# Leaving out the second half of short expert blocks, by a list, and moving the last odd block's output into the loop

## The chip, the cores and the metric

The kernel runs on one core of a Trainium2 chip. The metric is the device time of one execution in microseconds (us). Five engines work side by side, each with its own instruction queue: PE (matrix products; PEld, its weight loads, is listed apart), DVE (vector arithmetic), ACT (functions and copies), POOL (here: gathers, scatters and small loads through its DMA queue) and SP (transfers). They wait for one another through semaphores. An instruction that waits holds up everything behind it in its engine's queue.

## What is computed

Four layers on a tensor of 2048 tokens of 256 numbers, each adding an expert network's output to its input. Layers 0 to 2 are the ones in question:

```python
# layer 0: every token goes to the experts that hold the first 0.8 of the router's probability
h = relu(einsum('bth,ehf->betf', x, W1) + b1)      # 8 experts, 256 -> 1024
y = einsum('betf,efh->beth', h, W2) + b2           # 1024 -> 256
out = einsum('bte,beth->bth', gate, y)
# layer 1: every token goes to the expert of the largest logit, 256 -> 1024 -> 256, gelu
# layer 2: the same, 256 -> 512 -> 256, gelu
x = x + out
```

The router decides on the chip which tokens an expert gets. With the given inputs the tokens for each of the eight experts are 1250, 991, 1681, 916, 1881, 989, 825, 1662 in layer 0; 0, 0, 0, 0, 0, 1, 2046, 1 in layer 1; and 402, 238, 116, 124, 331, 278, 335, 224 in layer 2.

## The kernel before

**Blocks.** Each expert's tokens are sorted into blocks of 256 rows, that is two tiles of 128 rows; an expert's last block is filled up with rows that are dumped. That makes 43 blocks in layer 0, 10 in layer 1 and 12 in layer 2, 65 in all. A block is short when its second tile holds no token: an expert whose last block has 128 tokens or fewer. By the counts above these are blocks 27, 35 and 42 of layer 0 (42 is the last one, and 43 is odd), blocks 0 and 9 of layer 1 (9 is the last of an even number) and blocks 3, 4, 6, 8 and 10 of layer 2.

**What PE does with a block** (`blocks(L)`). `trans` turns the gathered rows, four transposes. `hidden` makes the hidden layer for both tiles at once, 256 columns wide; each product is three matmuls (lines 821 to 823) of a high and a low part, 48 matmuls in layers 0 and 1 and 24 in layer 2. `output` makes the second product, one tile of 128 tokens after the other (j = 0, 1): 24 matmuls for each tile in layers 0 and 1, 12 in layer 2.

**What the others do.** POOL gathers a block's rows (L711) and scatters the result, through L739 in layer 0 (`scatter_add`, which first waits at L723 until the scatter of the block before has landed) and through L729 in layers 1 and 2. ACT evaluates the hidden layer (L1435, L1436). DVE makes all low parts (L1671): of the first weights (`w1_lo`), the second weights (`w2_split`), the hidden layer (`lows`) and the block's inputs (`x_lo`); it then adds the bias to each output tile (`outputs`, L1938) and in layer 0 multiplies it by the gate (L1943).

**The order.** Blocks q = 2i + k go through a hardware loop over i with k = 0 and 1 written out in its body, one block of lookahead, and the loop's length fixed for the worst routing: iterations past the end are skipped by a branch (L956). Within iteration i PE's order is: hidden(i,1), trans(i+1,0), output(i,0), hidden(i+1,0), trans(i+1,1), output(i,1). So what follows output(q) on PE is the hidden layer of block q + 2, and its first matmul waits for x_lo(q + 2). DVE's order is: w1_lo of q + 2, w2_split and lows of q + 1, x_lo of q + 2, then outputs of q. An odd last block is left over: its second product stands behind the loop, after the skipped iterations, on PE (`output(pairs, 0)`) and on DVE (`outputs(pairs, 0)`).

**The lists.** The routing is turned into block and slot lists by a chain of small DVE operations, each waiting for the one before (`link`). It ends for the gathers with the list of slots (L1830), on which the first gather waits. PE, ACT, DVE, POOL and SP each read the number of blocks with a register load from SBUF (L417).

Of the kernel before, what the change touches and what calls it, by code (L numbers as in the profile page):

```python
# [67 lines left out]
def build(nc, t):  # L68

    with ExitStack() as ctx:  # L70
        def sb(name, shape, dt=F32):
            return ctx.enter_context(nc.sbuf_tensor(name, shape, dt))
# [52 lines left out]
        GBK = sb("block_gates", [P, 2, BTT])  # L125
        B2B = sb("b2_block", [P, 2, D])
        BLK = [sb(f"blocks{L}", [1, 64], I32) for L in SPARSE]


        ROWS = B * SEQ + DUMPS * P  # L130
# [687 lines left out]
        def _(pe):  # L818
# [88 lines left out]
            def blocks(L):  # L907
                NF = LAYERS[L][1] // P

                def trans(i, k):  # L910

                    first = isinstance(i, int) and i == 0
                    pe.wait_ge(s_xb[L][k], i * (16 * BTT) + 16 * BTT)
                    if not first:
                        pe.wait_ge(s_xlo[L], i * 2 + k - 1)
                    for m in range(KD):
                        for tt in range(BTT):
                            last = nc.tensor.transpose(PS[:, 6 + k, m * BT + tt * P:m * BT + (tt + 1) * P],  # L918
                                                       XBL[L][:, k, tt, m * P:(m + 1) * P], ident[:])
                    last.then_inc(s_xps[L], 1)  # L920

                def hidden(i, k, first=False):
                    q = i * 2 + k
                    pe.wait_ge(s_xlo[L], q + 1)
                    pe.wait_ge(s_w1sp[L], q + 1)
                    for f in range(NF):
                        if first and f == NF // 2:
                            trans(0, 1)
                        if not first or f >= 4:
                            pe.wait_ge(s_hhi[L], NF * q + (H0[L] + f - 3))  # L930
                        out = PS[:, f % 4, (f // 4) * BT:(f // 4 + 1) * BT]
                        for m in range(KD):
                            w = slice((m * NF + f) * P, (m * NF + f + 1) * P)
                            last = mm3(out, WB1[L][0][:, k, w], WB1[L][1][:, k, w], XTh[:, k, m, :], XTl[:, k, m, :],
                                       m == 0, m == KD - 1)
                        last.then_inc(s_hps[L], 1)

                def output(i, k):
                    q = i * 2 + k
                    pe.wait_ge(s_w2sp[L], q + 1)  # L940
                    pe.wait_ge(s_hlo[L], NF // 2 * (q + 1) + H0[L])
                    for j in range(BTT):
                        pe.wait_ge(s_yev[L], BTT * q + j + 1)
                        for f in range(NF):
                            tok = slice((f % 2) * BT + j * P, (f % 2) * BT + (j + 1) * P)
                            w = slice(f * D, (f + 1) * D)
                            last = mm3(PS[:, 4 + j, 0:D], HTh[:, k, f // 2, tok], HTl[:, k, f // 2, tok],
                                       WB2[L][0][:, k, w], WB2[L][1][:, k, w], f == 0, f == NF - 1)
                        last.then_inc(s_y[L], 1)

                pe.wait_ge(s_list, L + 1)
                steps, pairs, n = counts(pe, L)
                trans(0, 0)
                hidden(0, 0, True)
                with pe.Fori(0, STEPS[L]) as i:
                    with pe.If(i < pairs):  # L956
                        hidden(i, 1)
                        with pe.If(i + 1 < steps):
                            trans(i + 1, 0)
                        output(i, 0)  # L960
                        with pe.If(i + 1 < steps):
                            hidden(i + 1, 0)
                            with pe.If(i + 1 < pairs):
                                trans(i + 1, 1)
                        output(i, 1)
                with pe.If(pairs < steps):
                    output(pairs, 0)

            def ffn3():
                fh, fl = FEAT[3]  # L970
# [690 lines left out]
        def _(dve):  # L1661
            steps_done = [0]

            def link(ins):

                steps_done[0] += 1
                ins.then_inc(s_dve, 1)
                dve.wait_ge(s_dve, steps_done[0])
# [85 lines left out]
            def order(L):  # L1754
# [4 lines left out]
                et = "p (e t) -> p e t"  # L1759
                tmp = SC[:, 2, 0:ET].rearrange("p (t e) -> p t e", e=8)  # L1760
                cmp = SC[:, 2, ET:ET + 64].rearrange("p (e k) -> p e k", k=8)
                own, upto, even = (SC[:, 2, 256 + 8 * k:264 + 8 * k] for k in range(3))
                dve.wait_ge(s_rank, L + 1)

                link(nc.vector.tensor_copy(tot.rearrange(et, e=8),
# [7 lines left out]
                link(nc.vector.tensor_reduce(own, cmp, axis=AX.X, op=ALU.add))  # L1773
                link(nc.vector.tensor_tensor_scan(upto, ONE[:, 0:8], own, 0.0, ALU.mult, ALU.add))
                block_list(L, upto)
                nc.vector.tensor_tensor(own, upto, own, ALU.subtract)
                link(nc.vector.tensor_tensor(off, cum, tot, ALU.subtract))
                link(nc.vector.scalar_tensor_tensor(off.rearrange(et, e=8), own.unsqueeze(2).broadcast_to([P, 8, NT]),
# [20 lines left out]
                for c in range(NC):  # L1799
# [2 lines left out]
                    nc.vector.tensor_tensor(OHL[:, n, :].rearrange("p t (a o) -> p t a o", o=2), lane.unsqueeze(1).broadcast_to(pairs),  # L1802
                                            SLOP[:, n, :].unsqueeze(2).broadcast_to(pairs), ALU.is_equal).then_inc(s_inv, 1)

            def block_list(L, upto):
                n = BLOCKS[L]
                hit = SC[0:1, 6, 0:n * 8].rearrange("p (b e) -> p b e", e=8)
# [10 lines left out]
            def slot_tokens(L):  # L1818
# [3 lines left out]
                if L == 0:  # L1822
# [5 lines left out]
                                             empty.rearrange("p (g j) -> p g j", j=DUMPS),  # L1828
                                             DUMP[:].unsqueeze(1).broadcast_to([P, S // DUMPS, DUMPS]), ALU.mult))
                nc.vector.scalar_tensor_tensor(TOK[:, 0:S], inv, -1.0, empty, ALU.add, ALU.add).then_inc(s_tok, 1)  # L1830

            def order0():

# [3 lines left out]
                tot, cum, off = (SC[:, 5, k * ET:(k + 1) * ET] for k in range(3))  # L1837
                tmp = SC[:, 2, 0:ET].rearrange("p (t e) -> p t e", e=8)
                cmp = SC[:, 2, ET:ET + 64].rearrange("p (e k) -> p e k", k=8)
                own, upto, first = (SC[:, 2, 256 + 8 * k:264 + 8 * k] for k in range(3))  # L1840
                dve.wait_ge(s_rank, 1)
                link(nc.vector.tensor_copy(tot.rearrange(et, e=8),
                                           PS[:, 7, ET:2 * ET].rearrange("p (t e) -> p e t", e=8)))
# [17 lines left out]
                link(nc.vector.tensor_tensor(first, upto, own, ALU.subtract))  # L1861
                link(nc.vector.tensor_scalar(TGT, first[0:2 * LC], float(BTT), PIDC[0:2 * LC, 1:2], ALU.mult, ALU.add))
                link(nc.vector.tensor_copy(TGTB[:], TGT.unsqueeze(2).broadcast_to([2 * LC, 8, 2])))

                def columns(h):
                    T = NT // 2
# [32 lines left out]
            def blocks(L):  # L1899
# [67 lines left out]
                else:  # L1967
                    w2_lo(0, 0)
                with dve.Fori(0, STEPS[L]) as i:
                    with dve.If(i < pairs):  # L1970
                        with dve.If(i + 1 < steps):
                            w1_lo(i * 2 + 2, 0)
                        w2_split(i, 1)
                        lows(i * 2 + 1, 1)
                        with dve.If(i + 1 < steps):
                            x_lo(i * 2 + 2, 0)
                        outputs(i, 0)
                        with dve.If(i + 1 < steps):
# [5 lines left out]
                            lows(i * 2 + 2, 0)  # L1984
                            with dve.If(i + 1 < pairs):
                                x_lo(i * 2 + 3, 1)
                        outputs(i, 1)
                        if L == 0:
                            with dve.If(i + 1 < pairs):
                                gate_column(i + 1, 1)  # L1990
                with dve.If(pairs < steps):
                    outputs(pairs, 0)

            def add_back(L, n0, dh, dl):

# [748 lines left out]
```

## Time and profile before

| | |
|---|---|
| time before, median of 3 runs | 1180.87 us (1180.74 to 1182.09) |
| time of the profiled execution | 1182.63 us |
| its span in the trace | 1181.0 us |
| PE busy | 1020.3 us (86%), 7745 matmuls |
| DVE busy | 911.6 us (77%) |
| ACT busy | 641.6 us (54%) |
| POOL busy | 552.1 us (47%) |
| layer 0, 43 blocks | 80 to 611 us of the span |
| layer 1, 10 blocks | 691 to 824 us |
| layer 2, 12 blocks | 858 to 960 us |

The profiled execution is 1.76 us above the median, and its span is 1.63 us shorter than its time. Times within the span are counted from its start. PE's column of busy time counts pipelined matmuls, so a PE that is always busy is one that is never left without a matmul. "PEclk" is the granted clock of PE as a share of 2.4 GHz; 0.50 is 1.2 GHz. A row of a window gives its start and end, its length, then busy time and instructions of PE, PEld, DVE, ACT and POOL, the granted clock, the busy share of the DMA engines and GB/s. A row of a sequencer's operation gives its duration in ns (least, median, most) and when the first and the last began. In a timeline, where a row gives start and duration, the bracket behind an instruction gives its engine's idle time ahead of it and what ended that. A name with q behind an engine (PEldq, POOLq) is that engine's sequencer: loads of registers, branches and waits.

### The profile page before, as it was taken

The numbers are of one execution on the slowest core, as the hardware profiler recorded it, in microseconds if no ns is written. First come the engines' busy times: TensorE is split into PE (matmuls) and PEld (weight loads), VectorE is DVE, ScalarE is ACT, GpSimd is POOL, SyncE is SP. The second block draws the span as 40 slices with busy tenths as digits, with TensorE's granted clock in tenths as the row PEclk, the third lists the DMA queues.
The fourth block names the chain that finished last, engine by engine and source line by source line (L and its number), as shares of the span: only waits on it lengthen the run. The fifth ranks groups of instructions, "written<-read, shape, count | busy, mean of one in ns | idle before, by whom it ended". The sixth has DMA issues, their size and how long they took to land.

```text
span 1181.0 us, 26183 instructions
## 1 busy us (share of the span) xinstructions
PE 1020.3 (86%) x7745; PEld 967.1 (82%) x7745; DVE 911.6 (77%) x1565; ACT 641.6 (54%) x1388; POOL 552.1 (47%) x370
## 2 busy tenths in 40 slices
PE   6249999999999999999959749999859958889896
PEld 5239999999999999999956549998659946778785
DVE  7877888888888888888828768785748854867795
ACT  4227676767677767777615547672357625223321
POOL 1312888888888888888620044642047620000000
PEclk9568999999999999999976769999889979989998
DMA  7346787878787878787531267652368753030202
GB/s 212 116 170 206 225 242 217 246 228 243 216 250 224 246 215 247 227 246 215 145 62 37 70 225 259 231 186 83 105 218 257 238 161 114 14 90 24 95 14 72
DMA packets 84376, 203.50 MB, mean 172 GB/s; under 512 B 16626, under 2 KB 58114, under 8 KB 70754
## 3 DMA queue, kind: packets, MB, share of 16 engines
q1 hardware_dynamic: 60242, 159.35, 40.2%
q0 software_dynamic: 24080, 43.53, 15.3%
q8 instruction: 22, 0.36, 0.1%
q14 instruction: 32, 0.26, 0.1%
HBM read 168.36 MB, written 34.49 MB: 172 GB/s over the span
## 4 chain that ended last, share of the span: by engine, by line
PE 69%; DVE 11%; DMA 8%; issue 5%; ACT 3%; POOL 2%; POOLq 1%; SPq 1%; DVEq 0%; ACTq 0%
PE ps L821 22%; PE ps L822 21%; PE ps L823 21%; DMA y_rows<-w_raw,slot_rows 2%; PE ps L918 2%; DMA z_tok<-in_L_w 1%; PE ps L833 1%; DVE featA_lo L1671 1%; DVE hidden_lo L1671 1%; POOL w_raw L711 1%; DMA w_raw<-z_rows,slot_rows 1%; DMA z_tok<-y_rows 1%; DMA scratch<-in_L_w 1%; DVE x_tok L2000 1%; DMA z_rows<-z_tok 1%
## 5 line engine op out<-in xcount | busy, mean ns | idle before, releaser
L1435 ACT ACTIVATE hidden_f<-ps,b_block 128x256 f32<-128x256 f32 x472 | 240.8, 510 | 182.4 <-PE ps L823 179.6
L711 POOL DMA_INDIRECT x_tok<-z_gate_rows,slot_rows x86 | 236.1, 2745 | 121.7 <-DVE block_gates L1954 66.0
L1436 ACT ACTIVATE hidden_hi<-ps,b_block 128x256 fp32r<-128x256 f32 x472 | 242.6, 514 | 0.0
L821 PE MATMUL ps<-w_hi,featA_hi 128*128 128x256 f32 (+1 forms) x708 | 203.1, 287 | 9.5 <-DVE scratch L2349 6.3
L821 PE MATMUL ps<-featB_hi,hidden_hi 128*128 128x256 f32 x696 | 199.3, 286 | 7.1 <-issue 3.6
L822 PE MATMUL ps<-w_lo,featA_hi 128*128 128x256 f32 (+1 forms) x708 | 202.6, 286 | 0.0
L823 PE MATMUL ps<-w_hi,featA_lo 128*128 128x256 f32 (+1 forms) x708 | 202.5, 286 | 0.0
L822 PE MATMUL ps<-featB_lo,hidden_hi 128*128 128x256 f32 x696 | 195.8, 281 | 0.0
L823 PE MATMUL ps<-featB_hi,hidden_lo 128*128 128x256 f32 x696 | 195.2, 280 | 0.0
L1671 DVE TENSOR_TENSOR hidden_lo<-hidden_f,hidden_hi 128x512 fp32r<-128x512 f32 x272 | 175.2, 692 | 14.6 <-ACT hidden_hi L1436 13.3
L739 POOL DMA_INDIRECT x_rows<-w_raw,slot_rows x86 | 141.7, 1648 | 44.8 <-issue 25.0
L821 PEld LDWEIGHTS ps<-w_hi,featA_hi 128*128 128x128 f32 (+1 forms) x708 | 137.3, 194 | 11.1 <-issue 7.1
L821 PEld LDWEIGHTS ps<-featB_hi,hidden_hi 128*128 128x128 f32 x696 | 131.8, 189 | 7.9 <-DVE hidden_lo L1671 4.1
L823 PEld LDWEIGHTS ps<-w_hi,featA_lo 128*128 128x128 f32 (+1 forms) x708 | 137.6, 194 | 0.2
L822 PEld LDWEIGHTS ps<-w_lo,featA_hi 128*128 128x128 f32 (+1 forms) x708 | 137.5, 194 | 0.2
L823 PEld LDWEIGHTS ps<-featB_hi,hidden_lo 128*128 128x128 f32 x696 | 131.9, 189 | 0.0
L822 PEld LDWEIGHTS ps<-featB_lo,hidden_hi 128*128 128x128 f32 x696 | 131.7, 189 | 0.0
L711 POOL DMA_INDIRECT w_raw<-z_rows,slot_rows x44 | 53.5, 1215 | 155.2 <-DVE slot_rows L1830 74.9
L1938 DVE TENSOR_TENSOR w_raw<-ps,b_block 128x256 f32<-128x256 f32 x130 | 53.9, 419 | 68.2 <-PE ps L823 64.0
L821 PE MATMUL ps<-w_hi,featB_hi 128*128 128x256 f32 x288 | 84.5, 293 | 9.4 <-DVE w_lo L1671 6.5
L1671 DVE TENSOR_TENSOR featA_lo<-scratch,featA_hi 128x2048 fp32r<-128x2048 f32 (+3 forms) x49 | 89.4, 1824 | 2.6 <-ACT featA_hi L1559 1.3
L729 POOL DMA_INDIRECT y_rows<-w_raw,slot_rows x44 | 59.7, 1357 | 61.7 <-DVE w_raw L1938 47.5
(479 smaller groups left out, 2561.3 us busy)
## 6 DMA issues: line engine op xcount, KB each, us to landing
scratch<-in_L_w SPq DMA_DIRECT2D x53, 1024.0 KB, 5.2
z_tok<-in_L_w SPq DMA_DIRECT2D x32, 1024.0 KB, 8.2
x_tok<-in_L_w SPq DMA_DIRECT2D x21, 1024.0 KB, 5.0
b_block<-in_L_ffn_b POOLq DMA_DIRECT2D x65, 128.0 KB, 6.4
z_tok<-y_rows SPq DMA_DIRECT2D x12, 512.0 KB, 5.5
z_tok<-in_L_w SPq DMA_DIRECT2D x12, 512.0 KB, 5.3
scratch<-in_L_w SPq DMA_DIRECT2D x12, 512.0 KB, 5.2
z_rows<-z_tok SPq DMA_DIRECT2D x8, 512.0 KB, 2.9
```

Source lines behind the costliest of these rows:

```text
L711: gp.indirect_dma_start(XBL[L][:, k, tt, :], None, ZD if L else ZD0, bass.IndirectOffsetOnAxis(ap=TOK[:, q * BTT + tt:q * BTT + tt + 1], a ...
L729: gp.indirect_dma_start(YD, bass.IndirectOffsetOnAxis(ap=TOK[:, q * BTT + tt:q * BTT + tt + 1], axis=0), YB[:, k, tt, :], None).then_inc(s ...
L739: gp.indirect_dma_start(XD, bass.IndirectOffsetOnAxis(ap=TOK[:, q * BTT + tt:q * BTT + tt + 1], axis=0), YB[:, k, tt, :], None, compute_op ...
L821: nc.tensor.matmul(out, lh, rh, start=first, stop=False)
L822: nc.tensor.matmul(out, lh, rl, start=False, stop=False)
L823: return nc.tensor.matmul(out, ll, rh, start=False, stop=last)
L833: last = nc.tensor.transpose(PS[:, g % 4, j * P:(j + 1) * P], src[:, c * TPC + j, k * P:(k + 1) * P], ident[:])
L918: last = nc.tensor.transpose(PS[:, 6 + k, m * BT + tt * P:m * BT + (tt + 1) * P], XBL[L][:, k, tt, m * P:(m + 1) * P], ident[:])
L1435: act.activation(HF[:, f // 2, part], ps, func, bias=b1)
L1436: act.activation(HTh[:, k, f // 2, part], ps, func, bias=b1).then_inc(s_hhi[L], 1)
L1671: return nc.vector.tensor_tensor(out, full, hi.bitcast(F32), ALU.subtract)
L1938: nc.vector.tensor_tensor(YB[:, k, j, :], PS[:, 4 + j, 0:D], B2B[:, k, :], ALU.add).then_inc(s_yev[L], 1)
```

## The change

Three things are changed in layers 0 to 2.

DVE makes a list that says for each block whether its second tile is empty. `short_ends`, two linked operations, stands in the middle of the chain that makes the lists; `short_blocks`, three operations, follows at its end.

On PE, `output` loads the block's entry of that list into a register between the first and the second tile. If the block is short, the 24 (or 12) matmuls of the second tile are left out and one matmul of the same form takes their place, which only raises the semaphore and gives DVE defined values to read. The wait for the second tile's buffer now stands ahead of the branch. The other engines do the same work for a short block as before.

The output of an odd last block stands in the loop, in the iteration in which only k = 0 exists, on PE and on DVE; what stood behind the loop goes.

The core of the diff (the arrangement of DVE's loop follows PE's):

```diff
@@ PE, output(i, k)
-                    for j in range(BTT):
-                        pe.wait_ge(s_yev[L], BTT * q + j + 1)
+
+                    def tile(j):
                         for f in range(NF):
 ...
                         last.then_inc(s_y[L], 1)
 
+                    pe.wait_ge(s_yev[L], BTT * q + 1)
+                    tile(0)
+                    short = pe.value_load(SHORT[0:1, bass.ds(q, 1)], min_val=0, max_val=1)
+                    pe.wait_ge(s_yev[L], BTT * q + 2)
+                    with pe.If(short < 1):
+                        tile(1)
+                    with pe.Else():
+                        nc.tensor.matmul(PS[:, 5, 0:D], HTh[:, k, 0, P:2 * P], WB2[L][0][:, k, 0:D],
+                                         start=True, stop=True).then_inc(s_y[L], 1)
@@ PE, the loop
                 with pe.Fori(0, STEPS[L]) as i:
-                    with pe.If(i < pairs):
-                        hidden(i, 1)
+                    with pe.If(i < steps):
+                        with pe.If(i < pairs):
+                            hidden(i, 1)
                         with pe.If(i + 1 < steps):
                             trans(i + 1, 0)
                         output(i, 0)
                         with pe.If(i + 1 < steps):
                             hidden(i + 1, 0)
+                        with pe.If(i < pairs):
                             with pe.If(i + 1 < pairs):
                                 trans(i + 1, 1)
-                        output(i, 1)
-                with pe.If(pairs < steps):
-                    output(pairs, 0)
+                            output(i, 1)
@@ DVE, the list
+            def short_ends(own, upto, count, slack):
+
+                link(nc.vector.scalar_tensor_tensor(slack[0:1].unsqueeze(2), own[0:1].unsqueeze(2), float(BT), count[0:1],
+                                                    ALU.mult, ALU.subtract))
+                link(nc.vector.scalar_tensor_tensor(SEND[:], slack[0:1], float(P), upto[0:1], ALU.is_ge, ALU.mult))
+
+            def short_blocks(L):
+
+                n = BLOCKS[L]
+                room = HF[0:1].rearrange("p a c -> p (a c)")
+                hit, any_ = room[:, 0:n * 8].rearrange("p (b e) -> p b e", e=8), room[:, n * 8:n * 9]
+                link(nc.vector.tensor_tensor(hit, SEND[:].unsqueeze(1).broadcast_to([1, n, 8]),
+                                             IO[0:1, 1:n + 1].unsqueeze(2).broadcast_to([1, n, 8]), ALU.is_equal))
+                link(nc.vector.tensor_reduce(any_, hit, axis=AX.X, op=ALU.add))
+                nc.vector.tensor_scalar(SHORT[:, 0:n], any_, 1.0, None, ALU.min)
```

In `order` (layers 1 and 2) `short_ends` stands right behind `block_list`, in `order0` (layer 0) behind the two operations that turn the first block of each expert into targets. `short_blocks` is the last statement of `slot_tokens`, behind the operation at L1830 that raises the gathers' semaphore.

## Rows read from the trace of the kernel before

**Rows 1.** The page, part 1: busy us (share of the span) and instructions

```profile
PE 1020.3 (86%) x7745; PEld 967.1 (82%) x7745; DVE 911.6 (77%) x1565; ACT 641.6 (54%) x1388; POOL 552.1 (47%) x370
```

**Rows 2.** Windows inside layers 0, 1, 2 (columns as told above)

```profile
106.00:594.00 488.00, 488.00 (x4130) 488.00 (x4129) 420.82 (x538) 343.67 (x780) 388.78 (x201) 1.00 0.75 226
694.00:821.00 127.00, 122.68 (x997) 122.24 (x996) 92.57 (x98) 80.73 (x186) 57.20 (x46) 0.96 0.62 207
858.00:957.00 99.00, 78.79 (x658) 76.88 (x656) 71.47 (x106) 59.68 (x137) 62.59 (x60) 0.94 0.70 218
```

**Rows 3.** Timeline: PE, block 27's second tile, next hidden; start us, duration

```profile
428.58 0.28 PE L821 MATMUL ps<-featB_hi,hidden_hi 128*128 128x256 f32 x1
...
431.38 0.28 PE L821 MATMUL ps<-w_hi,featA_hi 128*128 128x256 f32 x1
```

**Rows 4.** Timeline: DVE in the same stretch, x_lo

```profile
429.83 0.68 DVE L1671 TENSOR_TENSOR w_lo<-ps,w_hi 128x512 fp32r<-128x512 f32 x1
```

**Rows 5.** Timeline: x_lo and the matmul it releases, in layer 2

```profile
884.04 0.68 DVE L1671 TENSOR_TENSOR w_lo<-ps,w_hi 128x512 fp32r<-128x512 f32 x1
884.85 0.38 PE L821 MATMUL ps<-w_hi,featB_hi 128*128 128x256 f32 x1 [2.07 <-DVE w_lo L1671]
```

**Rows 6.** One line's sequencer instructions, L955, window 429 to 429.7 us

```profile
L955 PEldq ALU_OP  x1: 32/32/32, 429.3 to 429.3; - x1
```

**Rows 7.** The same view: L417 (register load), L956; timeline of PE at 858

```profile
L417 PEldq TENSOR_LOAD <-blocks x3: 301/308/483, 80.1 to 858.4; - x3
L417 PEldq FUSED_REGOPS  x3: 151/151/165, 80.6 to 858.7; - x3
L956 PEldq COMPARE_BRANCH  x7: 208/208/208, 594.9 to 599.3; - x7
857.98 0.96 PE L903 MATMUL ps<-hidden_f 128*128 128x32 bf16 x32
```

**Rows 8.** Windows after two pauses of PE; timeline row of the first

```profile
1088.53 0.39 PE L821 MATMUL ps<-featB_hi 128*128 128x256 f32 x1 [1.90 <-DVE featB_lo L1671]
1089.08:1092.49 3.41, 3.41 (x18) 3.41 (x17) 1.54 (x4) 0.95 (x3) 0.00 (x0) 0.50 0.00 0
884.85:888.30 3.45, 3.45 (x29) 3.45 (x30) 2.35 (x4) 2.91 (x7) 2.66 (x2) 1.00 0.80 266
```

**Rows 9.** End of layer 0: timelines of PE, DVE, POOL; L723's waits

```profile
600.20 0.38 PE L821 MATMUL ps<-featB_hi,hidden_hi 128*128 128x256 f32 x1 [3.56 <-issue]
608.02 0.61 DVE L1943 TENSOR_SCALAR w_raw<-w_raw,block_gates 128x256 f32<-128x256 f32 x2
609.38 1.54 POOL L739 DMA_INDIRECT x_rows<-w_raw,slot_rows  x1 [7.54 <-DVE w_raw L1943]
L723 POOLq EVENT_SEMAPHORE  x2: 17/17/17, 594.6 to 604.1; - x2
```

**Rows 10.** Layer 1, block 0: timelines of DVE (x_lo of block 2), PE

```profile
717.09 0.68 DVE L1671 TENSOR_TENSOR w_lo<-ps,w_hi 128x512 fp32r<-128x512 f32 x1
...
720.29 0.28 PE L821 MATMUL ps<-w_hi,featB_hi 128*128 128x256 f32 x1
```

**Rows 11.** End of layer 1: timeline of POOL, block 9's scatters

```profile
818.90 0.96 POOL L729 DMA_INDIRECT y_rows<-w_raw,slot_rows  x1 [1.92 <-DVE w_raw L1938]
821.77 0.96 POOL L729 DMA_INDIRECT y_rows<-w_raw,slot_rows  x1 [1.92 <-DVE w_raw L1938]
```

**Rows 12.** Layer 2: timeline of POOL, one scatter

```profile
908.60 1.34 POOL L729 DMA_INDIRECT y_rows<-w_raw,slot_rows  x1 [3.15 <-DMA y_rows<-w_raw,slot_rows]
```

**Rows 13.** The lists: timelines of DVE (layer 0) and POOL (layer 1)

```profile
60.67 0.17 DVE L1860 TENSOR_TENSOR_SCAN scratch<-ones,scratch 128x8 f32<-128x8 f32 x1
60.88 0.17 DVE L1861 TENSOR_TENSOR scratch<-scratch 128x8 f32<-128x8 f32 x1
88.37 0.69 DVE L1671 TENSOR_TENSOR w_lo<-ps,w_hi 128x512 fp32r<-128x512 f32 x1 [5.01 <-ACT w_hi L1420]
687.68 1.03 POOL L711 DMA_INDIRECT w_raw<-z_rows,slot_rows  x1 [74.90 <-DVE slot_rows L1830]
```

More of the change, by code:

```diff
@@ L127, in build @@
         BLK = [sb(f"blocks{L}", [1, 64], I32) for L in SPARSE]
+        SHORT = sb("short_blocks", [1, 56], I32)
+        SEND = sb("short_block_end", [1, 8])
         ROWS = B * SEQ + DUMPS * P
@@ L1761, in order @@
                 cmp = SC[:, 2, ET:ET + 64].rearrange("p (e k) -> p e k", k=8)
-                own, upto, even = (SC[:, 2, 256 + 8 * k:264 + 8 * k] for k in range(3))
+                own, upto, even, slack = (SC[:, 2, 256 + 8 * k:264 + 8 * k] for k in range(4))
                 dve.wait_ge(s_rank, L + 1)
@@ L1775, in order @@
                 block_list(L, upto)
+                short_ends(own, upto, count, slack)
                 nc.vector.tensor_tensor(own, upto, own, ALU.subtract)
@@ L1830, in slot_tokens @@
                 nc.vector.scalar_tensor_tensor(TOK[:, 0:S], inv, -1.0, empty, ALU.add, ALU.add).then_inc(s_tok, 1)
+                short_blocks(L)
             def order0():
@@ L1839, in order0 @@
                 cmp = SC[:, 2, ET:ET + 64].rearrange("p (e k) -> p e k", k=8)
-                own, upto, first = (SC[:, 2, 256 + 8 * k:264 + 8 * k] for k in range(3))
+                own, upto, first, slack = (SC[:, 2, 256 + 8 * k:264 + 8 * k] for k in range(4))
                 dve.wait_ge(s_rank, 1)
@@ L1863, in order0 @@
                 link(nc.vector.tensor_copy(TGTB[:], TGT.unsqueeze(2).broadcast_to([2 * LC, 8, 2])))
+                short_ends(own, upto, count, slack)
                 def columns(h):
@@ L1969, in blocks @@
                 with dve.Fori(0, STEPS[L]) as i:
-                    with dve.If(i < pairs):
+                    with dve.If(i < steps):
                         with dve.If(i + 1 < steps):
                             w1_lo(i * 2 + 2, 0)
-                        w2_split(i, 1)
-                        lows(i * 2 + 1, 1)
+                        with dve.If(i < pairs):
+                            w2_split(i, 1)
+                            lows(i * 2 + 1, 1)
                         with dve.If(i + 1 < steps):
@@ L1986, in blocks @@
                                 x_lo(i * 2 + 3, 1)
[L1987 to L1992, printed above, removed]
+                        with dve.If(i < pairs):
+                            outputs(i, 1)
+                            if L == 0:
+                                with dve.If(i + 1 < pairs):
+                                    gate_column(i + 1, 1)
             def add_back(L, n0, dh, dl):
```

## The prediction

> **What bounds the kernel now.** I read the busy totals first and distrust them: PE is busy 86% of the span, the most of all [rows 1], but that is an average over stages with different limits. So I went on to windows inside each layer. In layer 0 PE is never without a matmul: 488.00 of 488.00 us at clock 1.00, 4130 matmuls, so 0.118 us each [rows 2]. In layer 1 PE is busy 97% and DVE 73%; in layer 2 PE 80%, DVE 72%, POOL 63%, and nobody is full [rows 2]. A product left out can therefore save its time in layer 0 and 1 at most, and only as far as the next thing on PE is ready. Which thing that is, I read from timelines around single short blocks, since that is where the change acts.
>
> **Part 1: second products left out.** A second tile is 24 matmuls, one of them replaced: 23 x 0.118 = 2.71 us freed on PE per short block of layers 0 and 1, and 11 x 0.118 = 1.30 in layer 2.
>
> *Layer 0, blocks 27 and 35.* Block 27's second tile starts at 428.58 and the next hidden layer at 431.38 [rows 3]. That hidden layer needs x_lo(29), which DVE does at 429.83 for 0.68, so until 430.51 [rows 4]. From the end of such an operation to the matmul that waited for it passes 884.85 - (884.04 + 0.68) = 0.13 us [rows 5]. So it can start at 430.64: the gain is 431.38 - 430.64 = 0.74 us, not 2.71.  Block 35 has the same pattern (the hidden layer 0.75 later than x_lo allows). Together 1.48; the bounds are 0 and 2 x 2.71 = 5.42.
>
> *Layer 1, block 0.* x_lo(2) ends at 717.09 + 0.68 = 717.77, plus 0.13 = 717.90; the hidden layer starts at 720.29 [rows 10]. Gain 2.39, nearly all of 2.71, because DVE is ahead here.
>
> *Layer 1, block 9, the last.* Nothing follows on PE; what follows is its second scatter. It began at 821.77, released by DVE's addition; the first began at 818.90 for 0.96 [rows 11]. With the second tile there at once, POOL can issue it behind the first: 818.90 + 0.96 + 0.30 (gap between issues) = 820.16. Gain 1.61.
>
> *Layer 2, five blocks.* POOL's scatters wait for the scatter before to land, 3.15 us in the row shown and alike three more times [rows 12], and PE waits 2.07 us for x_lo [rows 5]. PE stops early only to wait longer: gain 0. Bounds: +5 x 1.30 = 6.5 gained if PE leads after all, -5 x 0.21 = -1.0 if each jump shows [rows 7]. I take 0, by the row of POOL.
>
> **Part 2: the load and the branch on PE.** Each of 65 blocks gains a register load (0.31 for the load, 0.15 for the register operation behind it, up to 0.05 between them and an assert), a wait and a branch of 0.07 to 0.21 [rows 7]: about 1.05 us of sequencer time with the enclosing branches. It stands in front of the second tile, so PE's queue must hold more than that. The loop's back edge, which stands behind the last matmul of an iteration, was executed at 429.3 while those matmuls ran until 431.3 [rows 6, 3]: the sequencer is 2.0 us ahead. 1.05 fits, so I cost it at nothing; its cover is the queue of matmuls in front. If that cover is gone, each of the 53 blocks of layers 0 and 1 pays up to 1.05. The buffer wait that now stands before the branch is long satisfied in layer 0: DVE emptied that bank for the block before, and a hidden layer of 48 x 0.118 = 5.7 us lies between. Nothing else is queued behind it but PE's own next matmuls.
>
> **Part 3: the odd last block's output in the loop.** Before, PE walks 7 skipped iterations (branch at L956, seven of them from 594.9 to 599.3) and sits idle 3.56 us before block 42's output at 600.20; DVE's gates run at 608.02 for 0.61, and the scatter starts at 609.38 [rows 7, 9]. After, output(42) follows block 41's at once. PE ends 600.20 - 3.56 = 596.64; 24 matmuls x 0.118 = 2.8 make 599.5; addition and gates end by 601. Block 42 is short, so its second tile is there too. Then what is late next? The scatter must wait until block 41's has landed, which was at 604.1 [rows 9]. From the end of DVE's gates, 608.63, to the scatter's start passed 0.75; 604.1 + 0.75 to 0.9 gives 605.0. Gain 609.38 - 605.0 = 4.4 us. The second scatter and the reloading of rows behind it follow in a fixed chain. The skipped iterations now lie behind the output, under the scatter. Bounds 0 (block 41's landing is not earlier and something else waits) and 5.
>
> **Part 4: the list.** Linked operations on 8 numbers follow each other every 60.88 - 60.67 = 0.21 us [rows 13]. short_ends adds two, 0.42, to the chain that ends in the slot list. In layer 0 DVE goes through it without a gap; in layer 1 POOL's gather waited for exactly that list [rows 13]: +0.42 each. In layer 2 the gather waits for rows from DMA: 0. short_blocks (three operations, the first on 352 numbers; at the 0.69 us that 512 columns take it is at most 1.4 in all) comes behind the gather's release, in front of DVE's 5.01 us of waiting for ACT [rows 13]: 0; without that cover, 1.4.
>
> **The sum.** +0.42 + 0.42 - 1.48 - 2.39 - 1.61 - 4.4 + 0 = -9.0 us. On the profiled execution 1182.6 becomes 1173.6; on the median, 1180.87 - 9.0 = **1171.8**.
>
> **The rivals.**
>
> *The clock falls in the pauses.* Blocks 27 and 35 leave PE about 2.71 - 0.74 = 2.0 us without work, in a stage that so far had none. A pause of 1.90 us ahead of 1088.53 was followed by 3.41 us at 0.50, that is 1.2 GHz; the pause of 2.07 ahead of 884.85 was followed by clock 1.00 [rows 8, 5]. So it can go either way. At half clock 3.41 us do the work of 1.7: if both fall, 3.4 us are lost and the time is 1175.2. [...]
>
> *The end of layer 0 does not move*, because the reload of rows waits on something other than block 42's scatter: 1171.8 + 4.4 = 1176.2.
>
> *PE bounds everywhere.* Then all products left out count: 5 x 23 + 5 x 11 = 170 x 0.118 = 20.1 us, less 0.84 for the list: 1161.6. For it speaks PE's 86% [rows 1]; against it x_lo, done only at 430.51 [rows 4]. The Trainium skill (Perfetto Trace Analysis, Identifying the Most-Contended Engine) would have me take this case, since it says to work on the engine of highest occupancy; the row of x_lo is why I don't.
>
> *Slower: the load drains PE.* If the sequencer's load waits for the matmuls in flight, or the lead at this place is under 1.05 us, PE stands still in each of the 53 blocks of layers 0 and 1 for up to 0.9 us: +47.7, and 1180.87 - 9.0 + 47.7 = 1219.6. It decides from the point where load, wait and branch together exceed the lead of 2.0 us. Against it: the load at 858.4 took 0.31 to 0.48 and was over before the 32 small matmuls in flight, which ran from 857.98 to 858.94 [rows 7].
>
> *The list marks nothing*, and only the output has moved: 1180.87 + 0.84 - 4.4 = 1177.3.
>
> **How the numbers follow.** Forecast 0.50, clock 0.18, end of layer 0 unmoved 0.07, PE everywhere 0.09, slower 0.10, list empty 0.03, others 0.03. The range takes in the forecast with layer 2's bounds (1171.8 - 6.5 = 1165.3) and the two cases up to 1176.2, and ends at 1177.5: 1165 to 1177.5. Two tenths of a per cent, about what a measurement of this kernel can tell from no change, are 2.4 us. All cases but the slower one and some of the others are faster by more: 0.84; within it 0.05; slower 0.11.
>
> **What would show it.** Right: about 170 fewer matmuls; in the short blocks of layer 0 PE idle near 2 us with x_lo named as releaser, and the hidden layer 0.7 earlier; between first and second tile of ordinary blocks no gap; PE without a pause ahead of output(42) and the first of its scatters close behind the landing of block 41's; layer 1's PE gap under 0.5 us behind block 0. Wrong: idle "issue" time on PE in front of each second tile (the slower rival); windows of clock 0.50 behind blocks 27 and 35 (the clock rival); layer 2 shorter by several us.

## The result and the profile after

The changed kernel takes 1174.58 us (median of 9), the kernel before took 1181.35 beside it; the ratio is 0.9938, with a 95% interval of 0.9923 to 0.9954, that is 7.3 us less (5.4 to 9.1). In a later comparison (e9 below) it was 0.9940 (0.9923 to 0.9957). Forecast were 9.0 us less, with a range from 15.9 to 3.4 less. The profiled execution took 1175.38 us, its span is 1173.7.

The page of the changed kernel, part 1:

```profile
PE 1001.7 (85%) x7575; PEld 946.4 (81%) x7576; DVE 914.8 (78%) x1580; ACT 643.4 (55%) x1388; POOL 556.3 (47%) x370
```

The same windows as in [rows 2]; the work comes up to 8.4 us earlier there, so those of layers 1 and 2 show the pattern and not the length:

```profile
106.00:594.00 488.00, 484.41 (x4083) 484.02 (x4082) 421.06 (x537) 344.67 (x780) 389.00 (x201) 1.00 0.75 226
694.00:821.00 127.00, 118.68 (x963) 117.80 (x962) 93.78 (x105) 79.69 (x183) 55.25 (x44) 0.96 0.61 203
858.00:957.00 99.00, 74.70 (x577) 71.87 (x578) 72.40 (x106) 56.88 (x132) 62.57 (x57) 0.90 0.71 223
```

7745 - 7575 = 170 matmuls are gone, as counted, so the rival by which the list marks nothing falls. In layer 0 PE now has 488.00 - 484.41 = 3.6 us without a matmul: the two short blocks. The timelines of PE and DVE around block 27 in the changed kernel:

```profile
428.37 0.28 PE L825 MATMUL ps<-featB_hi,hidden_lo 128*128 128x256 f32 x1
428.48 0.28 PE L960 MATMUL ps<-featB_hi,hidden_hi 128*128 128x256 f32 x1
430.56 0.38 PE L823 MATMUL ps<-w_hi,featA_hi 128*128 128x256 f32 x1 [1.79 <-DVE w_lo L1683]
...
429.73 0.68 DVE L1683 TENSOR_TENSOR w_lo<-ps,w_hi 128x512 fp32r<-128x512 f32 x1
```

L960 is the one matmul that stands for the second tile. Behind it PE waits for x_lo (429.73 + 0.68 = 430.41, and 0.15 to the matmul), as forecast. The bracket counts the idle time from the modelled end of L960; from start to start, less the usual 0.118, the pause is 1.96 us, and that is how pauses are given from here on. The hidden layer comes 0.82 us earlier than in [rows 3], of which 0.10 was there before. Block 35 repeats it: from the start of its second tile to the next hidden layer it took 2.80 us before (523.14 to 525.94) and 2.08 after (522.42 to 524.50). But behind it the window in the second line follows:

```profile
524.50 0.38 PE L823 MATMUL ps<-w_hi,featA_hi 128*128 128x256 f32 x1 [1.79 <-DVE w_lo L1683]
...
525.60:529.01 3.41, 3.41 (x18) 3.41 (x18) 2.34 (x3) 2.52 (x6) 2.84 (x3) 0.50 1.02 345
```

For 3.41 us the granted clock is 0.50, 1.2 GHz: block 37's hidden layer takes 7.21 us from its first to its last matmul, where 5.63 are usual. The 1.58 us are more than the two blocks had gained (0.72 each).

The end of layer 0 in POOL's timeline; compare [rows 9]:

```profile
598.53 1.59 POOL L741 DMA_INDIRECT x_rows<-w_raw,slot_rows  x1 [5.48 <-DVE w_raw L1974]
600.43 1.67 POOL L741 DMA_INDIRECT x_rows<-w_raw,slot_rows  x1 [0.30 <-issue]
605.21 1.54 POOL L741 DMA_INDIRECT x_rows<-w_raw,slot_rows  x1 [3.12 <-DMA x_rows<-w_raw,slot_rows]
```

Block 42's first scatter starts at 605.21 in place of 609.38, and what releases it is no longer DVE but the landing of block 41's scatter (at 604.4 by the row of its wait): the wait that was forecast to be late next. Layer 1, in the timelines of PE and DVE at block 0 and of POOL at block 9 ([rows 10, 11]):

```profile
713.72 0.68 DVE L1683 TENSOR_TENSOR w_lo<-ps,w_hi 128x512 fp32r<-128x512 f32 x1
714.53 0.38 PE L823 MATMUL ps<-w_hi,featB_hi 128*128 128x256 f32 x1 [0.97 <-DVE w_lo L1683]
...
813.21 0.96 POOL L731 DMA_INDIRECT y_rows<-w_raw,slot_rows  x1 [1.92 <-DVE w_raw L1969]
814.48 0.96 POOL L731 DMA_INDIRECT y_rows<-w_raw,slot_rows  x1 [0.30 <-issue]
```

The last two scatters are 1.27 us apart, where they were 2.87. Behind block 0 PE pauses 1.14 us from start to start.

### The profile page after: what moved, and what is told of

Read it like the earlier page. It is cut to its first block, busy times and chain, and to the rows that moved or that the text cites. A ratio compares the mean times of both kernels' runs of the same rounds, so it can differ in the third digit from the quotient of the medians.

```text
span 1173.7 us, 26502 instructions
## 1 busy us (share of the span) xinstructions
PE 1001.7 (85%) x7575; PEld 946.4 (81%) x7576; DVE 914.8 (78%) x1580; ACT 643.4 (55%) x1388; POOL 556.3 (47%) x370
## 4 chain that ended last, share of the span: by engine, by line
PE 66%; DVE 14%; DMA 8%; issue 6%; ACT 3%; POOL 1%; DVEq 1%; POOLq 1%; SPq 0%; ACTq 0%
PE ps L823 20%; PE ps L824 20%; PE ps L825 20%; PE ps L920 2%; DMA y_rows<-w_raw,slot_rows 2%; DMA w_raw<-z_rows,slot_rows 2%; DVE hidden_lo L1683 1%; PE ps L835 1%; DVE featB_lo L1683 1%; DVE featA_lo L1683 1%; DVE x_tok L2031 1%; DMA z_tok<-y_rows 1%; POOL w_raw L713 1%; DMA x_rows<-w_raw,slot_rows 1%; DVE x_tok L2083 1%
## 5 line engine op out<-in xcount | busy, mean ns | idle before, releaser
L823 PE MATMUL ps<-featB_hi,hidden_hi 128*128 128x256 f32 x672 | 191.7, 285 | 3.4 <-DVE hidden_lo L1683 3.4
L824 PE MATMUL ps<-featB_lo,hidden_hi 128*128 128x256 f32 x672 | 188.4, 280 | 0.0
L825 PE MATMUL ps<-featB_hi,hidden_lo 128*128 128x256 f32 x672 | 187.8, 279 | 0.0
L823 PEld LDWEIGHTS ps<-featB_hi,hidden_hi 128*128 128x128 f32 x672 | 126.5, 188 | 4.0 <-DVE hidden_lo L1683 4.0
L713 POOL DMA_INDIRECT w_raw<-z_rows,slot_rows x44 | 57.0, 1295 | 153.2 <-DVE slot_rows L1859 75.3
L825 PEld LDWEIGHTS ps<-featB_hi,hidden_lo 128*128 128x128 f32 x672 | 126.7, 189 | 0.0
L824 PEld LDWEIGHTS ps<-featB_lo,hidden_hi 128*128 128x128 f32 x672 | 126.4, 188 | 0.0
L823 PE MATMUL ps<-w_hi,featB_hi 128*128 128x256 f32 x288 | 85.2, 296 | 10.6 <-DVE w_lo L1683 8.4
```

The costliest lines, as they stand in the source:

```text
L713: gp.indirect_dma_start(XBL[L][:, k, tt, :], None, ZD if L else ZD0, bass.IndirectOffsetOnAxis(ap=TOK[:, q * BTT + tt:q * BTT + tt + 1], a ...
L823: nc.tensor.matmul(out, lh, rh, start=first, stop=False)
L824: nc.tensor.matmul(out, lh, rl, start=False, stop=False)
L825: return nc.tensor.matmul(out, ll, rh, start=False, stop=last)
```

## The experiments

Each kernel was timed beside the kernel before. Where a total could not tell causes apart, stages of the profiled executions do; all are worked out from the starts of POOL's gathers and scatters in the timelines. "To 41" is the time from layer 0's first gather to block 41's first scatter, "41 to 42" from there to block 42's first, "layer 1" from its first gather to its last scatter, "falls" the stretches at clock 0.50 behind blocks 27 and 35; a dash stands where no second tile is left out in layer 0, and there the clock stays at 1.00 from 110 us to the end of block 41.

| kernel | ratio to before (95%) | to 41 | 41 to 42 | layer 1 | falls |
|---|---|---|---|---|---|
| before | 1 | 515.98 | 10.99 | 134.09 | - |
| the change | 0.9938 (0.9923 to 0.9954) | 516.10 | 6.68 | 130.45 | 35 |
| e9, the change again | 0.9940 (0.9923 to 0.9957) | 518.17 | 6.56 | 130.29 | 27, 35 |
| e1, move only | 0.9968 (0.9955 to 0.9981) | 516.00 | 6.59 | 133.79 | - |
| e2, skip only | 0.9977 (0.9961 to 0.9992) | 517.40 | 8.73 | 129.80 | 35 |
| e3, load but no skip | 0.9957 (0.9938 to 0.9976) | 515.96 | 6.55 | 132.13 | - |
| e8, no skip in layer 2 | 0.9948 (0.9931 to 0.9964) | 515.26 | 6.66 | 133.69 | none |
| e4, x_lo early | 0.9910 (0.9885 to 0.9935) | 511.43 | 6.64 | 130.40 | none |
| e10, x_lo early, no skip | 0.9955 (0.9940 to 0.9971) | 515.74 | 6.55 | 132.70 | - |
| e5, filler | 0.9901 (0.9884 to 0.9918) | 514.69 | 6.48 | 129.74 | none |
| e12, filler again | 0.9926 (0.9902 to 0.9950) | 514.57 | 6.58 | 130.25 | none |
| e11, half the filler | 0.9936 (0.9917 to 0.9955) | 513.98 | 6.60 | 132.55 | none |
| e6, one load more | 0.9942 (0.9922 to 0.9963) | 516.15 | 6.66 | 132.04 | 35 |
| e7, three loads more | 1.0384 (1.0362 to 1.0406) | 555.46 | 6.46 | 139.46 | 35 |

### The parts one by one

**e1_move_only**: the kernel before with the loops of PE and DVE as changed, and nothing else.

> Only the odd last block's output moves into the loop; no list, no load, no branch, every second product is made. Theory A (the end of layer 0 is a matter of order): block 42's whole output follows at 596.6 and takes 5.6 us, its gates end near 603.5, so the scatter still waits only for block 41's to land (604.1) and starts at 605.0 as in the changed kernel: -4.4 us, 1176.9 against 1181.3. Rival B (the end of layer 0 is shorter because block 42's second tile is left out): with all 48 matmuls in place at most 1 to 2 us are gained, 1179.5 or more.

Measured: 0.9968, on 1181.35 us 3.8 less. POOL's and DVE's timelines:

```profile
602.88 0.61 DVE L1943 TENSOR_SCALAR w_raw<-w_raw,block_gates 128x256 f32<-128x256 f32 x2
...
605.20 1.54 POOL L739 DMA_INDIRECT x_rows<-w_raw,slot_rows  x1 [3.14 <-DMA x_rows<-w_raw,slot_rows]
```

The gates end at 603.5 with all 48 matmuls in place and still wait for block 41's landing. From 41 to 42 the time is 4.4 us shorter: theory A, to the tenth; B falls.

**e2_skip_only**: the change without the move (and with a list of 58 in place of 56 entries).

```diff
-                    with pe.If(i < steps):
-                        with pe.If(i < pairs):
-                            hidden(i, 1)
+                    with pe.If(i < pairs):
+                        hidden(i, 1)
...
+                with pe.If(pairs < steps):
+                    output(pairs, 0)
```

> Only the second products of short blocks are left out, by the list; the odd last block's output stays behind the loop. Theory A: in layer 0 PE still idles about 3.6 us in the skipped iterations, but 24 matmuls fewer at the lower clock let the gates end about 3 us earlier (near 605.5) and the scatter start near 606.3 in place of 609.4; so either part alone takes most of the 4.4 us at this place, and the sum of the two runs' gains is larger than the whole change's: about -6.3, 1175 against 1181.3. Rival B (the move alone brings the 4.4): 1174.6 + 4.4 = 1179.

Measured: 0.9977, 2.7 us less: nearer to B. DVE and POOL:

```profile
608.15 0.76 DVE L1969 TENSOR_TENSOR w_raw<-ps,b_block 128x256 f32<-128x256 f32 x2 [7.47 <-PE ps L825]
...
610.18 1.54 POOL L741 DMA_INDIRECT x_rows<-w_raw,slot_rows  x1 [5.28 <-DVE w_raw L1974]
```

This execution runs 3.06 us behind that of before at this point (block 41's scatter at 601.45 against 598.39), so the scatter comes 2.26 us earlier, not 3.1. My slip: the half clock lay on block 42's first tile, which stays, and not on the second, so what is left out ran at full speed. The two runs' gains add up to 6.5 us, within their intervals the 7.3 of the whole; at this one place the move alone brings 4.40, the skip alone 2.26, both 4.31. So either part shortens this place, as A has it, and B, by which the left-out tile brings nothing here, does not hold at it. The total comes near B in part because layer 0 up to block 41 took 1.42 us longer than before (517.40), with a fall of the clock in it.

**e3_load_no_skip**: the list comes out as zero.

```diff
-                nc.vector.tensor_scalar(SHORT[:, 0:n], any_, 1.0, None, ALU.min)
+                nc.vector.tensor_scalar(SHORT[:, 0:n], any_, 0.0, None, ALU.min)
```

> The changed kernel with a list that is zero everywhere: list, register load, wait and branch stay, and no product is left out. Theory A: the 1.13 us that load and branch take on PE's sequencer lie behind the first tile's matmuls, so it differs from e1_move_only only by the list, +0.4 to +0.8: 1177.5. No idle time of PE between first and second tile. Rival C (load or branch costs PE something in each block): 0.2 us in 53 blocks would be +10.6, 1188; 0.9 us +48, 1225.

Measured: 0.9957, and 515.96 to block 41, the same as e1 and before to 0.04 us in 42 blocks. PE shows no idle time in layer 0. Load and branch cost nothing there; C falls. The list's 0.4 to 0.8 us are too small for the totals: e3 came out under e1, with intervals that overlap. So do those of e3 and of the change, so the 2.2 us between them, which is what all the left-out products bring in the totals, is not shown by the totals alone; the stages have to tell.

**e8_no_skip_layer2**: layer 2 goes back to two plain tiles.

> The changed kernel, but layer 2 makes all its second products, with no load and no branch there; layers 0 and 1 as changed. Theory A: in layer 2 the products left out are worth nothing, because POOL's scatters and x_lo end later: within 1 us of the changed kernel, 1174.6. Rival D (layer 2's five blocks save their time): 1174.6 + 6.4 = 1181. Rival E (they cost the 0.8 to 1.0 us by which layer 2 is longer in the changed kernel's trace): 1173.6, and layer 2 in this trace 0.8 to 1.0 us shorter than in the changed kernel's.

Measured: 0.9948, inside the interval of the change; D (1181, 0.9997) falls. From layer 2's first gather to its last scatter the traces of five kernels without skips there take 91.98, 92.39, 93.28, 93.89 and 94.04 us, those of the others (e7 aside) 92.46 to 96.34: no gain. E expected this trace 0.8 to 1.0 us shorter than that of the change; it is 0.5 longer (93.28 against 92.77), and executions differ by more than either.

### How deep the cover of the load is

**e6_one_more_load** and **e7_three_more_loads**: the load is repeated ahead of the one that is used.

```diff
+                    for _ in range(1):      # 3 in the other kernel
+                        pe.value_load(SHORT[0:1, bass.ds(q, 1)], min_val=0, max_val=1)
                     short = pe.value_load(SHORT[0:1, bass.ds(q, 1)], min_val=0, max_val=1)
```

> The changed kernel with the register load doubled, 0.6 us more of sequencer time in front of each second tile. Theory A (cover): from the start of the load to the last matmul of the first tile pass 2.08 us in layer 0; 1.13 + 0.6 = 1.73 fits, so nothing changes: 1174.6 within 1, PE not idle between first and second tile. Rival C (each load costs PE its time): +0.6 in 53 blocks, 1206.

> The changed kernel with the register load made four times. Theory A (cover of 2.08 us): 1.13 + 1.8 = 2.93 exceeds it by 0.85, so PE idles 0.8 to 0.9 us in front of each second tile of layers 0 and 1: about 50 blocks x 0.85 = +43, 1217. Rival C without a cover (1.8 us in each of 53 blocks): +95, 1270. Rival I (the cover is deeper than this place shows): no change.

Measured: 0.9942 with one more, nothing changed; 1.0384 with three more, 52 us above the change. The sequencer's own rows in the changed kernel at block 27 (the load, with the operation that works out its address, and the branch behind it):

```profile
L955 PEldq ALU_OP  x1: 36/36/36, 426.4 to 426.4; - x1
L955 PEldq TENSOR_LOAD <-short_blocks x1: 297/297/297, 426.5 to 426.5; - x1
L955 PEldq FUSED_REGOPS  x1: 151/151/151, 426.9 to 426.9; - x1
...
L957 PEldq COMPARE_BRANCH  x1: 220/220/220, 427.2 to 427.2; - x1
```

The load begins at 426.4 and the branch ends at 427.5, while the first tile's matmuls run until 428.48: 1.1 us of a cover of 2.1, the cover being the time for which the matmuls already queued keep PE busy. In e7 a load takes 0.64 us (they start at 299.4, 300.0, 300.7 and 301.3), and 1.1 + 3 x 0.64 = 3.0 exceeds the cover by 0.9. PE's timeline there at one second tile, and its group of the second products' first matmuls between 130 and 560 us:

```profile
302.20 0.38 PE L823 MATMUL ps<-featB_hi,hidden_hi 128*128 128x256 f32 x1 [0.67 <-issue]
```

```profile
L823 PE MATMUL ps<-featB_hi,hidden_hi 128*128 128x256 f32 x528 | 153.6, 291 | 22.1 <-issue 22.1
```

"issue" is PE waiting for its sequencer. The bracket's 0.67 again counts from a modelled end: the matmul before started at 301.26, so 0.94 us pass where 0.12 are usual, and 0.21 to the next. The group has 33 blocks with 0.67 each. To block 41 the time is 555.46 - 516.10 = 39.4 us longer than in the change (one fall of the clock in each), 0.94 for each of 42 blocks, against 0.85 forecast. So C (95 us) and I (none) fall. Layer 1 is 9.0 us longer and layer 2, which the forecast left out, 7.45 (100.22 in place of 92.77); 52 us in all, where 43 were forecast. One load is free here because it fits under the tile that is queued in front of it; four do not fit.

### What ends the pause

**e4_x_early** moves x_lo ahead of the hidden layer's low parts on DVE, for both values of k (one shown); **e10_x_early_no_skip** is the same with a list of zeros.

```diff
                             w2_split(i, 1)
-                            lows(i * 2 + 1, 1)
                         with dve.If(i + 1 < steps):
                             x_lo(i * 2 + 2, 0)
+                        with dve.If(i < pairs):
+                            lows(i * 2 + 1, 1)
                         outputs(i, 0)
```

> The changed kernel with one step moved on DVE: x_lo of block q + 2 stands ahead of the four low parts of block q + 1's hidden layer in place of behind them, in every block. Theory A (what follows a left-out tile waits for x_lo and for nothing else): its source is ready on ACT at 427.0 while DVE starts the four low parts at 427.3, so x_lo ends near 427.9, before the first tile's product ends at 428.5: the pauses of 1.96 us in blocks 27 and 35 and of 1.14 in layer 1's block 0 are gone, and with them the stretch of lower clock behind block 35 (1.6): -6.6 us against the changed kernel, 1168. Rival F (something else is late next, the first weights' low part or ACT's hidden layer): pauses stay above 1 us, 1173 to 1175. Rival G (the four low parts, now 0.6 us later, hold up ACT or the output in ordinary blocks): slower than 1176.

> x_lo early as in e4_x_early, but the list is zero everywhere, so no product is left out. Theory A (moving x_lo only removes the wait behind a left-out tile; where no tile is left out PE waits for nothing): the same as e3_load_no_skip, ratio 0.9957, 1177.6 against 1182.8; layer 0 up to block 41's scatter within 0.3 us of that run's 516.0. Rival J (x_lo early is faster by itself, in each block): layer 0 shorter by 1 us or more, ratio 0.992 or less, and then it explains part of what e4_x_early gained.

Measured: e10 differs from e3 by nothing (0.9955 and 0.9957; 515.74 and 515.96), so J falls. With the skip it is 0.9910, and block 41 comes after 511.43 us. DVE and PE at block 27:

```profile
427.37 0.68 DVE L1683 TENSOR_TENSOR w_lo<-ps,w_hi 128x512 fp32r<-128x512 f32 x1
...
428.70 0.28 PE L960 MATMUL ps<-featB_hi,hidden_hi 128*128 128x256 f32 x1
428.82 0.36 PE L823 MATMUL ps<-w_hi,featA_hi 128*128 128x256 f32 x1
```

x_lo is done at 428.05, and PE goes on without a pause. So x_lo was what PE waited for, and F, pauses above 1 us, falls. A little comes late next: the hidden layer behind it takes 6.18 us in place of 5.73 (its later matmuls wait for ACT), which leaves 3.2 of the 3.9 us of the two pauses, counted from the 514.6 of traces where the clock did not fall, and 4.7 counted from the change's own 516.10. This is the shortest layer 0 of all. The total is 10.6 us under before (7.7 to 13.6), 3.3 under the change where 6.6 were expected; its interval and the change's overlap, so what is shown is the stage.

### What the pause costs

**e5_warm**, **e12_warm_again** and **e11_warm_half** fill the pause in layer 0 with matmuls whose result nobody reads; **e9_after_again** is the change unaltered.

```diff
+                        for _ in range(16 if L == 0 else 0):      # 7 in e11
+                            nc.tensor.matmul(PS[:, 5, 0:D], HTh[:, k, 0, P:2 * P], WB2[L][0][:, k, 0:D],
+                                             start=True, stop=True)
                         nc.tensor.matmul(PS[:, 5, 0:D], HTh[:, k, 0, P:2 * P], WB2[L][0][:, k, 0:D],
```

> The changed kernel with 16 more matmuls of the same form ahead of the one that replaces a second tile in layer 0 (17 x 0.118 = 2.0 us, as long as the pause). Theory A (the pause of 1.96 us behind block 35 let the clock fall, which cost 1.6 us): PE has no pause there, the clock stays at 1.00 to the end of layer 0, hidden layers start as early as in the changed kernel: block 37's hidden layer takes 5.6 in place of 7.2 us, 1173.0 against 1174.6. Rival H (the clock fell for another reason than the pause): it falls there all the same, 1174.6.

> The changed kernel unaltered, on the same chip as the three beside it, so that they can be compared with it. Its ratio before was 0.9938; theory A and every rival expect 0.993 to 0.9945 again, and in its trace a pause of 1.96 us behind blocks 27 and 35, with the clock falling behind one of them or behind none, as it did in four traces so far (behind 35 in three of them, behind 27 in none).

> Filler as in e5_warm, but 7 matmuls in place of 16: the pause behind blocks 27 and 35 shrinks from 1.96 to about 1.1 us. Theory A (a pause about 2 us long can let the clock fall, a shorter one does so less): hidden layers start as before, no stretch at 0.50 within layer 0, layer 0 up to block 41's scatter 514.7 as in e5_warm. Rival H (any pause behind block 35 lets it fall): 516.1 as in the changed kernel.

> The kernel of e5_warm again, beside the changed kernel on one chip. e5_warm was 5 us under e6_one_more_load of its call, while its layer 0 accounts for 1.6. Theory A: the rest was chance in the later stages; here it is 1.6 us under e9_after_again (between 0.5 and 3). Rival K (the filler brings 4 to 5 us, by an effect outside layer 0): 4 us or more under e9_after_again, and the same stages behind layer 0 shorter in its trace again.

Windows behind blocks 27 and 35, two of e9_after_again, two of e8_no_skip_layer2 (whose layer 0 is the change's) and two of e12_warm_again, the last as long as a hidden layer:

```profile
432.80:436.21 3.41, 3.41 (x17) 3.41 (x18) 2.35 (x6) 1.56 (x4) 2.85 (x3) 0.50 1.01 337
528.37:531.78 3.41, 3.41 (x18) 3.41 (x17) 2.34 (x5) 1.68 (x4) 2.83 (x3) 0.50 1.04 326
```

```profile
432.76:436.17 3.41, 3.41 (x28) 3.41 (x29) 2.35 (x6) 2.24 (x7) 2.85 (x3) 1.00 0.99 319
526.74:530.15 3.41, 3.41 (x28) 3.41 (x29) 2.35 (x6) 2.24 (x7) 2.84 (x3) 1.00 0.94 332
```

```profile
430.72:436.45 5.73, 5.73 (x49) 5.73 (x48) 4.60 (x7) 4.56 (x13) 5.10 (x3) 1.00 1.03 310
524.66:530.39 5.73, 5.73 (x49) 5.73 (x48) 4.61 (x7) 4.56 (x13) 5.11 (x3) 1.00 1.02 313
```

With the same pauses of 1.94 to 1.96 us the clock falls twice (e9), once (the change, e2, e6) or not at all (e8): 5 falls behind 10 pauses in five traces (e7, where loads change the pause, is not counted). Where PE has no such pause there (before, e1, e3, e10, e4, e5, e12) it falls at none of the 14 places. The hidden layer behind the pause tells the price: 7.21 to 7.23 us from its first to its last matmul with a fall, 5.73 without, so 1.5 us each. The stages agree in the main: to block 41 it takes 514.57 and 514.69 with filler and no fall, 516.10 and 516.15 with one; in the three traces whose first gather starts late, near 84 us, 515.26 with none (e8), 517.40 with one (e2) and 518.17 with two (e9), so 2.1 us for the first and 0.8 for the second. e9's own expectation that it falls behind one block or none was wrong, and with it the thought that block 27 is safe. With half the filler, a pause of 1.13 us is left in both blocks, and the clock held in that trace (513.98, of which some is a better start of layer 0); two pauses alone would not show that, since the longer ones were passed half the time too. So the pause is the cause and filling it the cure; H falls.

The same happens in layer 1, which is easily overlooked. Its block 0 leaves a pause of 0.9 to 1.2 us in five traces (the change, e2, e5, e9, e12), and the clock stays at 1.00 behind it. In e11, e6 and e8 the pause is 2.4, 2.7 and 3.4 us, and the clock falls behind all three. There the 24 matmuls ahead of block 0's output took 2.9 us, in the five 4.3 to 4.4, at the lower clock for the most part; PE came sooner and waited longer. PE's first matmul behind the pause and a window in e6, and the window in e8:

```profile
713.67 0.38 PE L823 MATMUL ps<-w_hi,featB_hi 128*128 128x256 f32 x1 [2.53 <-DVE w_lo L1685]
714.00:717.41 3.41, 3.41 (x19) 3.41 (x18) 1.92 (x2) 3.20 (x5) 2.57 (x3) 0.50 0.98 329
716.87:722.50 5.63, 5.63 (x26) 5.63 (x27) 4.39 (x5) 4.33 (x8) 2.57 (x3) 0.50 0.94 359
```

These three have the long layers 1 of the table: 132.04 to 133.69 us, where the others with the skip (e7 aside) take 129.74 to 130.45. No run changes that pause alone, so here the link is what the traces have in common, not a test.

e5's total was 5 us under e6, measured together, where layer 0 explains 1.5. In the two traces, whose spans are 4.3 us apart, layer 1 is 2.3 us shorter in e5, as it is without the fall of the clock that e6 has there, and the last stage 2.4; the filler stands in neither. Beside the change on one chip the same kernel is 1173.47 against 1176.68 us, 0.9926 against 0.9940, with intervals that overlap: 3.2 us less, just beyond A's 0.5 to 3 and short of K's 4. K is not borne out, and not excluded below some 3 us either; the last stage, from layer 2's last scatter to the end, which nothing here touches, varies between 224.2 and 230.0 us among the traces.

## Why the prediction was right, point by point

The sum first. Between the two profiled executions the stages differ, in order, by 0.02 (to the first gather), 0.12 (to block 41's first scatter), -4.31, 0.52 (to layer 1's first gather), -3.64 (layer 1), -1.13 (to layer 2's first gather), 0.79 (layer 2) and 0.33 us (to the end), together -7.3. The forecast of 9.0 less lies inside the interval of 5.4 to 9.1, and the largest term, the end of layer 0, came as forecast. The -1.13 was not forecast; that stage takes 39.1 to 40.7 us among the traces.

**Layer 0, blocks 27 and 35.** Forecast 0.74 and 0.75; measured 0.72 each. The hidden layer behind the pause then takes 5.73 us in place of 5.63, so 0.10 of each is lost again. The step (read when the next thing is ready, not how much is removed) held, and e4 shows that it was that thing.

**The clock.** It was priced as a rival at 1.7 us for each fall and 0.18 for both. It belonged in the sum: with two pauses and rows that went either way, half a fall on each, 1.7 us, was the fair term. Then the sum is -7.3. That this is the measured figure is luck, since layer 1's term was too large as well: with the measured 1.5 for a fall and 2.2 in place of 4.0 for layer 1 it is -5.7, at the low end of the interval. In e9, with both falls, the two blocks lose 3.0 us and gain 1.4. The windows at 0.50, which the prediction named as a sign of being wrong, did come.

**Layer 0's end.** Forecast 4.4 and the scatter at 605.0; measured 605.21, and 4.31 from block 41 to 42. e1 shows that the place of the output in the order is enough for it (4.40, with all products made); the product left out would bring 2.26 by itself (e2) and adds nothing to the move. The rival by which the end of layer 0 does not move falls: from block 42's first scatter to layer 1's first gather pass 78.30 us before and 78.82 after.

**Layer 1, block 0.** Forecast 2.39; from the first transpose to block 2's hidden layer it took 27.35 us before and 25.87 after, 1.48 less. x_lo ended the wait as said, 0.13 us ahead. Mis-sized was the distance between PE and x_lo, which was taken from a single execution: x_lo(2) ended 24.83 us behind the first transpose there and 25.74 in the change, where block 1's transposes came 0.90 later, with PE waiting 0.50 us for their rows. The gap behind block 0 was to be under 0.5 us; it is 1.14, so this sign failed. PE's own part varies too: its first block of layer 1 took 21.5 us before and 21.7 in the change, both with 24 matmuls of block 1's hidden layer in 4.3 us, at the lower clock for the most part. In e3, without any skip, these took 2.9 and the whole 19.9, and block 2's hidden layer began 0.13 us behind x_lo, as soon as it does when it waits for it: there the skip can bring nothing. In nine traces with the skip layer 1 takes 131.0 us on average, in four without it 133.2: 2.2 gained, where 4.0 were forecast for blocks 0 and 9 together. The two groups overlap (129.74 to 133.69 and 132.13 to 134.09); the fall of the clock behind block 0 parts the first one: 130.2 on average in the six traces without it, 132.8 in the three with it.

**Layer 1, block 9.** Forecast 1.61, measured 2.87 - 1.27 = 1.60, and the same distance in every other trace with the skip.

**Layer 2.** Forecast 0; borne out by e8. The row of POOL stood on little: of the 24 scatters before only four waited for a landing, 3.15 us once and 1.72 to 1.75 three times, and three were released by DVE's addition. The rival by which PE bounds everywhere, so that all 170 products count (1161.6), falls. The Trainium skill (Perfetto Trace Analysis, Identifying the Most-Contended Engine) says to work on the engine of highest occupancy first. That is PE here (86%), and 170 matmuls less on it brought 7.3 us, of which 4.3 came from the order of its work.

**The list.** Forecast 0.42 in each of layers 0 and 1. The added operations in DVE's timeline of layer 1:

```profile
677.19 0.15 DVE L1820 SCALAR_TENSOR_TENSOR scratch<-scratch 1x8 f32<-1x8 f32 x1
677.38 0.15 DVE L1822 SCALAR_TENSOR_TENSOR short_block_end<-scratch 1x8 f32<-1x8 f32 x1
677.57 0.17 DVE L1789 TENSOR_TENSOR scratch<-scratch 128x8 f32<-128x8 f32 x1
```

Two operations, 0.38 us. Layer 1's gather comes 3.65 us earlier where the chain began 4.05 earlier: 0.40. In layer 0 they stand in the chain just so (0.38), but the chain began 0.40 sooner in this execution, so the first gather shows no difference.

**The load on PE.** Forecast 1.05 us under 2.0; measured 1.1 under 2.1 at block 27, and no cost in e3 and e6. The slower rival falls.

## What to carry to other kernels

What a product left out is worth is the time until the next operand on its engine is ready: 0.7 of 2.7 us in layer 0, until x_lo was moved ahead of work that nobody waited for yet (e4). A pause that a change opens on PE in a stage that had none must be priced with the clock, and can be filled (e5, e12). A register load and a branch cost PE nothing here as far as the matmuls queued ahead of them reached, and that reach can be measured by repeating the load until the time moves (e6, e7).

## What was not expected of the hardware

That a pause of the same length (1.94 to 1.96 us), at the same place, is followed by 1.2 GHz in one execution and not in another: behind block 27 in e9 and not in the change, which is the same program, and 5 times of 10 over five traces whose kernels have the same work there, at 1.5 us each.
